# A mixed token model on one core: filling products between the stages given up, those in the front and in the LSTM's steps kept

## The reference, cut to what matters

```python
x = x + L0_conv(ln(x))     # a memory MLP trained by gradient steps over T = 16 rows, then applied to q
t = t + L0_ffn(ln(t))      # a router: softmax over 8 experts, top 2, each expert 64 -> 256 (gelu) -> 64
x = x + L1_conv(ln(x))     # 1x1 conv, relu, 3x3 conv (4 dependent slices), relu, 1x1 conv in a chain
t = t + L1_ffn(ln(t))      # an LSTM over 256 tokens, for 4 images at once

def step(carry, xs):       # the LSTM, 256 times, each step needs the h of the one before
    i, f, g, o = gates(xs + h @ V)
    c_new = h * c + i * g
    h_new = o * tanh(c_new)
```

## Time and profile before

| | us |
|---|---|
| median of 3 runs | 555.31 (551.38, 555.31, 555.84) |
| the profiled execution, its own time | 553.62 |
| its span, first to last instruction | 551.8 |
| PE busy / DVE / ACT / GpSimd | 480.0 / 293.9 / 226.0 / 110.0 |
| granted TensorE clock, mean over the span | 0.985 |

### The profile page before, as it was taken

One profiled execution on the slowest core, in us unless ns is written; L12 is line 12 of the kernel. 1 busy time (PEld: TensorE's weight loads), 2 busy tenths in 40 slices (PEclk: granted clock), 3 DMA queues, 4 the chain that ended last, 5 costly groups with the idle time before them and its releaser, 6 DMA issues.

```text
span 551.8 us, 11229 instructions
## 1 busy us (share of the span) xinstructions
PE 480.0 (87%) x3973; PEld 298.0 (54%) x3973; DVE 293.9 (53%) x1366; ACT 226.0 (41%) x1125; POOL 110.0 (20%) x109
## 2 busy tenths in 40 slices
PE   7899999999998998998777999778888888888886
PEld 3688888888765234855543777333333333333333
DVE  3966666766746755055556444664444444444443
ACT  2365555655335641035543334333333333333332
POOL 4378777777310000003200000000000000000000
PEclk9899999999998999989999999999999999999999
DMA  7600000000000000000000000000000000000000
GB/s 223 265 1 1 2 1 1 2 0 2 1 1 0 1 2 1 0 1 2 1 2 2 1 2 1 1 1 1 2 1 2 2 1 1 2 1 2 2 1 20
DMA packets 3081, 7.68 MB, mean 14 GB/s; under 512 B 1484, under 2 KB 2065, under 8 KB 2833
## 3 DMA queue, kind: packets, MB, share of 16 engines
q1 hardware_dynamic: 3026, 6.97, 3.7%
HBM read 6.71 MB, written 0.26 MB: 13 GB/s over the span
## 4 chain that ended last, share of the span: by engine, by line
PE 55%; DVE 23%; ACT 14%; issue 7%; DMA 0%; DVEq 0%; ACTq 0%
PE bk L707 12%; DVE bk L1498 8%; ACT gi L1062 6%; DVE mem L1501 6%; PE bk L666 6%; ACT bk L1066 6%; PE bk L347 3%; PE bk L846 3%; PE bk L515 2%; PE bk L610 2%; PE bk L592 2%; PE bk L496 2%; PE bk L474 2%; PE bk L484 2%; PE bk L399 2%
## 5 line engine op out<-in xcount | busy, mean ns | idle before, releaser
L846 PE MATMUL bk<-idle 128*64 128x512 bf16 (+1 forms) x665 | 178.9, 372 | 0.0
L707 PEld LDWEIGHTS bk<-mem,lvh 65*64 65x64 f32 x1536 | 80.0, 136 | 148.5 <-DVE mem L1501 146.2
L707 PE MATMUL bk<-mem,lvh 65*64 65x4 f32 x1536 | 102.4, 205 | 50.4 <-DVE mem L1501 50.1
L1498 DVE TENSOR_TENSOR_SCAN bk<-gi 64x12 f32<-64x12 f32 x256 | 53.8, 210 | 98.1 <-ACT gi L1062 96.1
L1062 ACT ACTIVATE gi<-bk 128x4 f32<-128x4 f32 x256 | 44.9, 175 | 135.8 <-PE bk L707 135.4
L1501 DVE SCALAR_TENSOR_TENSOR mem<-og,bk 64x4 f32<-64x4 f32 x256 | 38.4, 150 | 53.7 <-ACT bk L1066 53.7
L846 PEld LDWEIGHTS bk<-idle 128*64 128x64 bf16 x665 | 57.1, 111 | 16.8 <-issue 2.8
L1066 ACT ACTIVATE bk<-bk 64x4 f32<-64x4 f32 x256 | 36.6, 143 | 50.6 <-DVE bk L1498 50.6
L1505 DVE SCALAR_TENSOR_TENSOR gi<-mem,bk 64x4 f32<-64x4 f32 x255 | 39.1, 153 | 8.8
L1064 ACT ACTIVATE og<-bk 64x4 f32<-64x4 f32 x256 | 42.6, 167 | 0.0
L1152 DVE TENSOR_TENSOR mem<-mem,bk 128x256 f32<-128x256 f32 x64 | 27.0, 421 | 17.2 <-PE bk L392 11.4
(11 more groups left out here) (318 smaller groups left out, 761.6 us busy)
## 6 DMA issues: line engine op xcount, KB each, us to landing
cw<-in_cw SPq DMA_DIRECT2D x1, 3456.0 KB, 12.5
w<-in_w SPq DMA_DIRECT2D x1, 520.0 KB
mem<-in_memw SPq DMA_DIRECT2D x1, 512.0 KB, 3.6
w1g<-in_w1g SPq DMA_DIRECT2D x1, 512.0 KB
w<-in_w SPq DMA_DIRECT2D x1, 512.0 KB
xm<-in_xm SPq DMA_DIRECT2D x1, 256.0 KB, 2.7
xs<-in_x SPq DMA_DIRECT2D x1, 256.0 KB, 4.0
out<-xs SPq DMA_DIRECT2D x1, 256.0 KB, 2.0
```

Source lines behind the costliest of these rows:

```text
L707: return nc.tensor.matmul(bk[row:row + D, 2 * (s // CH % 2) + k, c:c + B], lvh[:, g, :], hist[:, s, :], start=False, stop=True, skip_group ...
L846: nc.tensor.matmul(bk[64:128, 1, 0:n], idle[:, 0:D], idle[:, 128:128 + n], start=True, stop=True)
L1498: nc.vector.tensor_tensor_scan(c_t.rearrange("p b k -> p (b k)"), gi[0:D, 0:3 * B], gi[D:2 * D, 2:2 + 3 * B], 0.0, ALU.mult, ALU.add).then ...
```

## The change

One table of counts changes. Every entry but `AFTER[2]` becomes 0, so 8 + 8 + 3 + 20 + 4 + 28 = 71 filling products of 512 columns go. No other instruction, wait, buffer or transfer changes on any engine; PE's list is the only one that differs.

```diff
-AFTER = (8, 8, 10, 3, 0, 20, 4, 28)
+AFTER = (0, 0, 10, 0, 0, 0, 0, 0)
```

## The result

| | before | changed |
|---|---|---|
| median, 14 runs each | 555.58 (551.38 to 561.11) | 561.89 (559.07 to 566.24) |
| ratio, 95% interval | | 1.0131 (1.0096 to 1.0166) |
| profiled execution (its span) | 553.62 (551.8) | 566.24 (564.5) |
| granted clock, mean over the profiled span | 0.985 | 0.939 |

The account below looks back on a forecast made before the run. The prediction took the kernel as bound by dependencies passing between engines, PE the largest part. Its terms 0.0 - 0.3 + 0.95 + 0.7 gave +1.4 us on the 555.31 median, 556.7 us, range 552.0 to 560.5.

Parts of the forecast that it names:

- The gains of the gaps: Time saved in five gaps where fillers ran past PE's data, if the clock stayed full: 4.2 us in sum.
- (a): Behind the gradient loop: line 532 starts sooner, a gain of 0.9 us, with no clock lost there.
- (c): Experts' end: gain 0.65 us; together with (d), half clock costs 2.1 against a gain of 1.15, net +0.95.
- (d): Ahead of the convolution's taps: gain 0.5 us, but taps begin at half clock; net +0.95 together with (c).
- (e): Third norm and LSTM's start: gain 0.5 us, but half clock costs 1.4; taken +0.7, bounds -0.9 and +1.8.
- (b): Second norm and router: gain 1.6 us, eaten with (a)'s by half clock (0.0); later low stretch partly spared, -0.3.
- R3: Rival: the LSTM starts at half clock and stays there, 0.9 us more per step; 561.2 us; chance 0.08.
- R1: Rival: transposes at lines 564 and 573 count as work, clock back at 167; 554.8 us; chance 0.20.
- R2: Rival: the clock hardly falls, so all 4.2 us of gain arrive; 551.1 us; chance 0.12.

Follow-up runs that it names:

- a2: Kernel of before without the 20 + 4 fillers around the experts' end and the 1x1 products (convolution's start): 1.0026 of before.
- The trimmed kernels: Fillers in every gap, but only as many as end with PE's data: 0.9969 of before; with 7 more among the bias products 0.9954, then 6 at the router 0.9958.
- a3: Kernel of before without the 8 + 3 fillers around the second norm's transposes (router): 1.0009 of before.
- b1: Changed kernel with the third norm's 28 fillers put back: 1.0035 of before.
- b3: Changed kernel with the second norm's (router's) 8 + 3 fillers put back: 1.0122 of before.
- c1: Kernel of before without the fillers of both the convolution's start and the third norm: 1.0133 of before.
- c3: Changed kernel with the fillers inside the first 24 LSTM steps widened from 256 to 512 columns: 1.0119 of before.
- d2: Kernel of before without the 24 fillers at the convolution's start, timed again in a later round: 1.0052 of before.
- d3: Kernel of before without the fillers of both the convolution's start and the third norm, timed again: 1.0126 of before.
- d1: Kernel of before without the third norm's 28 fillers, timed again in a later round: 1.0009 of before.

## Why the prediction was wrong, step by step

- **The gains of the gaps** (4.2 us at full clock): right in mechanism, too large in size. (a) is 0.6 in the traces and not 0.9, since line 532 takes 0.26 us longer once PE starts it from idle. (c) is about 0.4 of 0.65 (line 629 to 652: 39.07 us in before, 38.66 in a2). The trimmed kernels, where the clock held, show 0.4 of 0.5 for (d) and 0.3 of 0.5 for (e). The 1.6 of (b) cannot be read alone, since half clock stood in it wherever these fillers were taken out. The timed runs gave 2.9 to 3.6 in all.
- **(b), the router** (0.0 and -0.3, bounds -2.5 to +1.0 and -1.7 to +1.0): right as a sum, within what a3 can tell: 1.0009 (0.9977 to 1.0040). Half clock lasted to line 592 and on, and the transposes did not end it. One part of it was wrong: I took 0.9 us as spared at the low stretch of 177.2, but line 629 to 652 is only 0.3 us shorter in a3, whose half clock ends ahead of line 629, than in before. What I missed, that line 558 itself may run at half clock and hold ACT, strikes kernels with and without the fillers.
- **(c) and (d), the convolution: the term that was mis-sized.** Taken +0.95, with 2.1 us of loss against 1.15 of gain. In the traces lines 652 to 685 took 3.0 to 4.1 us more, against a gain of 0.4 to 0.6 ahead of line 652: net about +3. With the 0.5 of gap (d), which lies inside these lines, the loss by itself is 3.5 to 4.6. Nine profiles had no fillers here (the changed kernel twice, a2, b1, b3, c1, c3, d2, d3); eight show 10.2 us of half clock and d3 13.7. I had put one stretch of 3.4 us mostly on the taps. In the changed kernel's profile the clock fell at 219.6, in the wait for the norm, stayed at 0.50 through the transposes (220.99) and the 1x1 products (223.46), and was back only at 229.8, with 4.3 us of taps behind it: three stretches in a row. So my upper bound of 3.7 was near the lowest loss that was measured. In timed runs the gap alone is worth +0.26 and +0.52%.
- **(e), the LSTM's start: mechanism right, size and end wrong.** I took +0.7 against the profile of before, with the clock full after 249. It was 10.2 us of half clock at best (24 steps in 36.3 us against 35.5 in that profile, and +0.5 ahead of them, less 0.1), and 17 to 24 us in the changed kernel's first profile, b3, c1 and d1 (38.5 to 39.4): +1.2 to +4.3, where my upper bound was 1.8. Against kernels whose clock held there (34.9) it is +1.8 to +4.9. I had also taken the step from 245.54 as 0.9 us longer for half clock, from its 2.09 against the 1.21 of the one before it. But they are different steps: at full clock this one takes 1.46 (a2, a3, d2), so before paid 0.6.
- **The rival R3 was the nearest.** It said that half clock stays on through the first steps, and the first profile shows that, with 20 us more of it than before; four of the nine profiles without these fillers have 17 us or more. I gave it 0.08, because in before the same steps had won the clock back in 3.4 us. That was one sample. That its 561.2 us was near the measured time is luck: some 3 us came from the convolution, which R3 left out, and its price of 0.9 a step was too high (4.5 us over the 9 steps behind the first new h in the longest stretch, every third of which took 1.95 us at either clock).
- **R1 and R2** fell: the clock was at 0.50 in lines 573 and 579, in the taps and at the LSTM's start.
- **The range** took "part of the bounds" as unlikely together. Its ends do not follow from the bounds it names, and even all the worst ones together (6.3 us) give 561.6, still under the measured 561.89. So the bounds of (c), (d) and (e) themselves were too tight. Both turn on one question, how long half clock lasts once PE goes idle, and I answered it too low in both places.

The Trainium skill's rule ("TensorE: Matmul & The Clock Gate", section "Why this matters for your kernels") against long idle gaps between bursts holds here: the 3.8 and 5.5 us gaps are the costly ones, and the short ones cost nothing that the timed runs can show. The same page of the Trainium skill, section "HAM oscillation — how this bites in real kernels", describes a matmul loop whose bursts are shorter than the waits between them, with waits long enough to lose the clock, so that each burst starts at half clock. The traces agree for the 1x1 products behind the 3.8 us wait, which ran at 0.50 in all nine of these profiles.

## What to carry to other kernels

In this kernel a filler costs about the time that it runs past the data PE waits for, and what it buys is the clock of the work *behind* the gap: so size each group to end with the wait (0.3% here, at the edge of the noise) and try some where real work is light though not idle (0.46% in all, clear of it). When fillers go, do not count one low stretch per gap: light work behind a long gap did not end the half clock here, and 3.8 us of idling brought 10.2 us of it. 1 us of half clock went with 0.26 to 0.33 us of time, by lines through the four rounds of before. And judge by many runs with their mean clock: one profile of the same kernel may have 10 us or 24 us of half clock at the same place.

## What was not expected of the hardware

- The same LSTM steps hold full clock when they have it and may not win it back: in the changed kernel's first profile half clock lasted 23.9 us through steps that in before ran at 1.00 from 248.9 on.
- Half clock came in pieces of 3.4 us and their multiples, at places that differ from run to run of one kernel: two profiles of the changed kernel had 13.6 and 6.8 us of it ahead of line 532, where 154.1 and 150.9 us had passed. Dips of 3.4 us, two of them twice as long, also appeared in the LSTM steps behind 275 us in twelve of the eighteen profiles, where nothing in the program differs from kernel to kernel.
- Two groups of fillers whose loss alone costs 1 to 3 us cost 7 together (c1, d3), and no trace here tells why.
